# Cross attention: the copies of the two transposed halves change engines and places

## The chip, the cores and the metric

One core of a Trainium2 chip runs the whole kernel. The metric is the device time of one execution in microseconds; the time of a kernel is the median over its runs.

## The reference

The kernel computes twelve residual blocks over `x` of 128 sequences, 32 tokens and 128 features. Three of them are cross attentions of 16 heads of 8 features, in which the 32 tokens of a sequence ask a context of 257 keys. They run the function that is changed here, and differ only in the mask that is added to the scores:

```
x = x + L1_xattn(ctx, ctx, layernorm(x), mask, ...)       # one mask for all
x = x + L2_xattn(layernorm(x), ctx, ctx, key_weights, ...) # + log(weights) per key
x = x + L3_xattn(layernorm(x), ctx, tokens, 0, ...)        # keys of token 0 masked

scores = einsum('bhqd,bhkd->bhqk', Q, K) / sqrt(8) + mask
attn = softmax(scores, axis=-1)
out  = einsum('bhqk,bhkd->bhqd', attn, V)  @ Wo + bo
```

## The kernel before, in words

`xattn(name)` is called for `x1`, `x2` and `x3`. It loops over the 128 sequences, called blocks. One block has 32 tokens and 16 heads, so 512 rows of scores, in four groups of 128 partitions (an index h runs over the groups); each row has 257 keys. The keys are split for the second product into two transposed halves of 128 and one last key, which is treated apart.

The work on a block is a pipeline over several iterations. Each engine runs its own list of stages, written out by hand, in one fixed order per iteration x; the loop body is unrolled eight times, with a part before and after it. The order inside an engine is the order of the code; between engines only semaphores hold. In iteration x the engines do:

- PE: the four transposes of the first half of block x-4 into PSUM bank 6 (L1695), the four of the second half into bank 7 (L1702), K of block x into bank 4 (L1708), V of block x into bank 5 (L1711). Then it waits until bank 7 has been copied out, because three products write into the same bank: the output product (L1721, one iteration in four), the products for the last key (L1729, one iteration in four) and the product with V of block x-5 (L1740, every iteration). Last come the scores of block x-1 into banks 0 to 3 (L1751).
- DVE: four reductions of block x-2 (L1804; each adds the mask to one bank, writes the scores to SBUF and takes their maximum), with the reciprocal of the sums of block x-3 (L1816) and the copy of bank 6 for block x-4 (L1821) between the second and the third; in `x3` the masked `kT` (L1829); in two iterations of four a sum for `oT` (L1836); the evacuation of the product with V (L1846); then what follows L1721 (L1855) or L1729 (L1859).
- ACT: the four exponentials of block x-2 (L1761), the copy of bank 7 for block x-4 (L1770) between the first and the second; `kT` of block x with its bias (L1778, not in `x3`); `vs` of block x (L1781).
- POOL: the head-masked queries `qb` (L1661), the last key's weights `PB` (L1669), the scaling of a block's exponentials by the reciprocals (L1676), which releases PE's transposes.
- SP: the loads of context, mask rows and keep rows, four blocks deep.

The waits that touch the change: `pT_psum` and `pT2_psum` say that bank 6 and bank 7 hold their transposes, `pT_ready` and `pT2_ready` that they are copied into `pt`; `s_summed` counts the reductions, `exp_done` the blocks of exponentials, `av_psum` the products with V.

Of the kernel before, what the change touches and what calls it, by code (L numbers as in the profile page):

```python
# [147 lines left out]
def program(nc, T, out):  # L148

    with ExitStack() as ctx:  # L150
# [4 lines left out]
        B = [ctx.enter_context(nc.psum_tensor(f"bank{i}", [P, 512], F32)) for i in range(8)]  # L155
# [1419 lines left out]
        def xattn(name):  # L1575

            bias = name != "x3"
            with ExitStack() as c2:
# [15 lines left out]
                pt = sb2("pt", [P, 2, 2, 4 * P])  # L1594
# [160 lines left out]
                @block.scalar  # L1755
                def _(act):
                    def stages(x, r_, i, ok):
                        def exps(b, hs, j):
                            for h in hs:
                                act.wait_ge(*s_summed(4 * b + h + 1))  # L1760
                                ins = act.activation(sx[:, j, h, 0:KEYS], sx[:, j, h, 0:KEYS], ACT.Exp, bias=nm[:, j, h:h + 1], scale=-1.0,  # L1761
                                                     accum_out=sm[:, j, h:h + 1])
                            return ins
                        if ok(x - 2):
                            exps(x - 2, (0,), (r_ - 2) % 4)
                        b, q = x - 4, r_ % 2
                        if ok(b):
                            act.wait_ge(*pT2_psum(b + 1))
                            act.wait_ge(*av_psum(b - 1))
                            act.copy(pt[:, q, 1, :], B[7][:]).then_inc(pT2_ready.sem, 1)  # L1770
                        if ok(x - 2):
                            exps(x - 2, (1, 2, 3), (r_ - 2) % 4).then_inc(exp_done.sem, 1)
                        b, q = x, r_ % 2
                        if ok(b):
                            if keep is None:
                                act.wait_ge(*k_psum(b + 1))
                                act.wait_ge(*scores(4 * (b - 1)))
                                act.activation(kT[:, q, :], B[4][:, 0:KEYS], ACT.Identity, bias=v(name + "_bk")).then_inc(k_ready.sem, 1)  # L1778
                            act.wait_ge(*kv_psum(b + 1))
                            act.wait_ge(*av_psum(b - 7))  # L1780
                            act.copy(vs[:, r_, :], B[5][:, 0:2 * P]).then_inc(v_ready.sem, 1)  # L1781
                    run(act, stages)

                @block.vector
                def _(dve):
                    st_ = Steps(dve, sig, "dve_step")
                    dve.wait_ge(*last_psum(1))
                    st_.count(dve.tensor_copy(VL[:], B[7][:, 0:NB]))
                    st_.link(dve.tensor_copy(bor[:], B[7][:, P:2 * P]))
                    st_.link(dve.tensor_tensor(X[:], X[:], bor[:].unsqueeze(1).to_broadcast([P, TILES, P]), ALU.add))  # L1790
                    dve.sem_inc(last_ready.sem, 1)  # L1791
                    if name == "x1":
                        dve.wait_ge(*row_loaded(4))
                        st_.link(dve.tensor_scalar(maskq[:], maskq[:], -1.0e9, None, ALU.mult))

                    def stages(x, r_, i, ok):
                        def reduce(b, j, hs):
                            add = maskq[:] if rows is None else rows[j][:]
                            for h in hs:
                                dve.wait_ge(*scores(4 * b + h + 1))  # L1800

                                dve.sem_inc(sig.sems["dve_passed"], 1)

                                dve.tensor_tensor_reduce(sx[:, j, h, 0:KEYS], B[h][:, 0:KEYS], add, -1.0, 3.0e38, ALU.add, ALU.min,  # L1804
                                                         nm[:, j, h:h + 1]).then_inc(s_summed.sem, 1)
                        b, j = x - 2, (r_ - 2) % 4
                        if ok(b):

                            dve.wait_ge(*pT2_psum(b - 3))
                            dve.wait_ge(*pb_ready(b - 3))  # L1810
                            reduce(b, j, (0, 1))
                        b, j = x - 3, (r_ - 3) % 4
                        if ok(b):
                            dve.wait_ge(*exp_done(b + 1))
                            dve.wait_ge(*p_ready(b - 3))
                            dve.reciprocal(rs[:, j, :], sm[:, j, :]).then_inc(rs_ready.sem, 1)  # L1816
                        b, q = x - 4, r_ % 2
                        if ok(b):
                            dve.wait_ge(*pT_psum(b + 1))
                            dve.wait_ge(*av_psum(b - 1))  # L1820
                            dve.tensor_copy(pt[:, q, 0, :], B[6][:]).then_inc(pT_ready.sem, 1)  # L1821
                        if ok(x - 2):
                            reduce(x - 2, (r_ - 2) % 4, (2, 3))
                        b, q, j = x, r_ % 2, r_ % 4
                        if ok(b):
                            if keep is not None:
                                dve.wait_ge(*k_psum(b + 1))
                                dve.wait_ge(*scores(4 * (b - 1)))
                                dve.tensor_tensor(kT[:, q, :], B[4][:, 0:KEYS], keep[j][:], ALU.mult).then_inc(k_ready.sem, 1)  # L1829
                        for half, late in ((0, 9), (1, 10)):  # L1830
                            if r_ % 4 == late % 4 and ok(x - late):
                                tl, tq = (x - late) // 4 if isinstance(x, int) else i * (U // 4) + (r_ - late) // 4, (r_ - late) % 8 // 4
                                dve.wait_ge(*a_ready(4 * (tl + 1)))
                                dve.wait_ge(*pl_ready(tl + 1))
                                dve.wait_ge(*y_psum(tl))
                                ins = dve.tensor_reduce(oT[:, half * 2 * S:(half + 1) * 2 * S].rearrange("p (b s) -> p b s", b=2),  # L1836
                                                        a[:, tq, 2 * half:2 * half + 2].rearrange("p b j s -> p b s j"), AX.X, ALU.add)
                                if half:
                                    ins.then_inc(o_ready.sem, 1)
                        b, q, tq = x - 5, (r_ - 5) % 4, (r_ - 5) % 8 // 4  # L1840
                        if ok(b):
                            dve.wait_ge(*av_psum(b + 1))
                            if q == 0:
                                dve.wait_ge(*o_ready((b // 4 if isinstance(b, int) else i * (U // 4) + (r_ - 5) // 4) - 1))

                            dve.scalar_tensor_tensor(out=a[:, tq, q, 0:4, :],  # L1846
                                                     in0=B[7][:, 2 * P:3 * P].rearrange("p (j s) -> p j s", j=4),
                                                     scalar=v(name + "_bv" if bias else "zero"),
                                                     in1=const("head").unsqueeze(2).to_broadcast([P, 4, S]),
                                                     op0=ALU.add, op1=ALU.mult).then_inc(a_ready.sem, 1)  # L1850
                        if r_ % 4 == 3 and ok(x - 11):
                            tl = (x - 11) // 4 if isinstance(x, int) else i * (U // 4) + (r_ - 11) // 4
                            dve.wait_ge(*y_psum(tl + 1))
                            xt_ = X[:, bass.ds(tl, 1), :]
                            dve.tensor_tensor(xt_, xt_, B[7][:, P:2 * P].unsqueeze(1), ALU.add).then_inc(x_added.sem, 1)  # L1855
                        if r_ % 4 == 0 and ok(x - 8):
                            tl, tq = (x - 8) // 4 if isinstance(x, int) else i * (U // 4) + (r_ - 8) // 4, (r_ - 8) % 8 // 4
                            dve.wait_ge(*pl_psum(tl + 1))
                            dve.tensor_tensor(a[:, tq, :, 4, :], B[7][:, 0:P].rearrange("p (b s) -> p b s", b=4),  # L1859
                                              VL[:, bass.ds(tl * 4, 4)].unsqueeze(2).to_broadcast([P, 4, S]), ALU.mult).then_inc(pl_ready.sem, 1)  # L1860
                    run(dve, stages)
                    st_.close()

# [321 lines left out]
```

## Time and profile before

| | |
|---|---|
| median of 3 runs | 3520.45 us (3514.63 to 3530.14) |
| the profiled execution, its time | 3534.02 us |
| its span | 3532.2 us |
| PE busy | 2646.5 us (75%) |
| DVE busy | 2237.4 us (63%) |
| ACT busy | 1821.8 us (52%) |
| POOL busy | 1673.7 us (47%) |
| granted TensorE clock, mean | 0.856 |

The scores (L1751) of the three cross attentions start between 815.1 and 1243.7, 1661.5 and 2091.8, and 2636.9 and 3066.4 us of the span. The busy shares of the table are means over stages with other limits; the rows below are read from the three stretches. In a timeline each row has its start, its duration, the engine, the line and the operation, and in brackets the idle time of the engine before it and what ended it. An instruction on DVE or ACT can start up to 0.1 us before the recorded end of the one before it, so steps are taken from start to start.

### The profile page before, as it was taken

How to read it: one execution, taken by the hardware profiler on the slowest of the kernel's cores; microseconds unless marked ns; L12 is line 12 of the kernel's file. 1: busy time of each engine (PE TensorE's matmuls, PEld its weight loads, DVE VectorE, ACT ScalarE, POOL GpSimd, SP SyncE). 2: the span in 40 equal slices, each digit the busy share in tenths (PEclk: the TensorE clock that was granted, in tenths of full speed). 3: DMA queues.
4: the chain of work that ended last, by engine and by line, in shares of the span. 5: the costliest groups of instructions: out<-in, count | busy, mean ns of one | idle time of the engine just before them, and what ended most of it. 6: DMA issues, size and time to landing. Idle time of an engine off the chain costs nothing. (4 is left out here: it accounts for less than half of the span.)

```text
span 3532.2 us, 96857 instructions
## 1 busy us (share of the span) xinstructions
PE 2646.5 (75%) x27184; PEld 2121.3 (60%) x27185; DVE 2237.4 (63%) x8001; ACT 1821.8 (52%) x5775; POOL 1673.7 (47%) x1776
## 2 busy tenths in 40 slices
PE   4972577738999979847999973477749999787562
PEld 2752466626777769825777751376627777566551
DVE  4876711147888847754888877431159999878415
ACT  3441033327999933224999975023338888644110
POOL 2630055525777710001777762035527777646161
PEclk9985588969999979968999996579979999999565
DMA  2003044331111100010333320223434545300122
GB/s 83 1 1 100 14 122 119 113 91 42 39 39 39 36 8 0 31 83 27 79 78 78 78 47 6 52 86 117 115 86 118 116 116 116 75 1 1 49 84 67
DMA packets 209741, 224.97 MB, mean 64 GB/s; under 512 B 29652, under 2 KB 177620, under 8 KB 208949
## 3 DMA queue, kind: packets, MB, share of 16 engines
q1 hardware_dynamic: 196948, 197.56, 21.2%
q0 software_dynamic: 12672, 25.98, 2.9%
q8 instruction: 55, 0.90, 0.1%
q14 instruction: 66, 0.53, 0.0%
HBM read 201.68 MB, written 21.76 MB: 63 GB/s over the span
## 5 line engine op out<-in xcount | busy, mean ns | idle before, releaser
L1676 POOL TENSOR_TENSOR sx<-sx,rs 128x1028 f32<-128x1028 f32 x384 | 731.2, 1904 | 297.4 <-DVE rs L1816 297.3
L1761 ACT ACTIVATE sx<-sx,nm 128x257 f32<-128x257 f32 x1536 | 770.7, 505 | 126.0 <-DVE nm L1804 115.2
L1804 DVE CUSTOM_DVE_ANT_0 sx<-bank,rows 128x257 f32<-128x257 f32 x1024 | 393.9, 422 | 63.5 <-PE bank L1751 48.0
L1438 ACT ACTIVATE hT<-bank,B 128x128 f32<-128x128 f32 x714 | 205.5, 367 | 432.2 <-PE bank L1406 285.4
L309 POOL TENSOR_TENSOR rstd<-var,nhalf 128x16 f32<-128x16 f32 x24 | 69.7, 2904 | 654.0 <-DVE var L326 654.0
L1464 DVE TENSOR_TENSOR yb<-bank,b2s 128x128 f32<-128x128 f32 x159 | 46.4, 292 | 425.4 <-remote 218.3
L1761 ACT ACTIVATION_READ_ACCUMULATOR sx<-sx,nm 128x1 f32 x1536 | 290.4, 189 | 0.0
L1751 PE MATMUL bank<-kT,qb 32*128 32x257 f32 x3072 | 275.9, 428 | 2.7 <-DVE nm L1804 2.5
L1419 PE MATMUL bank<-W,hT 128*128 x1428 | 231.7, 309 | 59.4 <-ACT hT L1438 42.1
L1740 PE MATMUL bank<-pt,vs 128*32 128x128 f32 x6144 | 245.6, 276 | 19.6 <-ACT pt L1770 6.2
L1821 DVE COPY pt<-bank 128x512 f32<-128x512 f32 x384 | 253.6, 660 | 2.1 <-PE bank L1695 1.7
L1695 PE MATMUL bank<-C,sx 128*128 128x128 f32 x1536 | 251.9, 286 | 2.9 <-POOL sx L1676 2.9
L1419 PEld LDWEIGHTS bank<-W,hT 128*128 128x128 f32 x1428 | 202.0, 216 | 77.1 <-issue 73.7
L1711 PEld LDWEIGHTS bank<-W,ct 128*128 128x128 f32 x1536 | 235.0, 193 | 22.1 <-ACT vs L1781 1.2
L1708 PE MATMUL bank<-ct,W 128*128 128x257 f32 x768 | 235.3, 388 | 16.7 <-DVEq L1791 15.3
L1406 PE MATMUL bank<-xT,W 128*128 128x128 f32 x1428 | 238.9, 317 | 0.7 <-DMA W<-in_L_w 0.5
L1695 PEld LDWEIGHTS bank<-C,sx 128*128 128x128 f32 x1536 | 161.0, 141 | 130.6 <-issue 100.7
L1711 PE MATMUL bank<-W,ct 128*128 128x128 f32 x1536 | 236.2, 277 | 0.2 <-ACT vs L1781 0.2
L1702 PE MATMUL bank<-C,sx 128*128 128x128 f32 x1536 | 230.6, 273 | 0.0
L1804 DVE CUSTOM_DVE_ANT_0 sx<-bank,maskq 128x257 f32<-128x257 f32 x512 | 196.4, 422 | 41.0 <-PE bank L1751 32.8
L1770 ACT COPY pt<-bank 128x512 f32<-128x512 f32 x384 | 217.1, 565 | 10.1 <-PE bank L1702 10.1
L1406 PEld LDWEIGHTS bank<-xT,W 128*128 128x128 f32 x1428 | 209.9, 224 | 11.6 <-issue 3.8
(384 smaller groups left out, 5798.6 us busy)
## 6 DMA issues: line engine op xcount, KB each, us to landing
ct<-in_ctxT SPq DMA_DIRECT2D x384, 128.5 KB
W<-in_L_w SPq DMA_DIRECT2D x159, 256.0 KB
rows<-rows_x SPq DMA_DIRECT2D x256, 128.5 KB
keep<-rows_keep SPq DMA_DIRECT2D x128, 128.5 KB
yg<-copy_outs SPq DMA_DIRECT2D x40, 256.0 KB
token_rows<-XN SPq DMA_DIRECT2D x24, 256.0 KB, 2.3
W<-in_L_w SPq DMA_DIRECT2D x39, 128.0 KB
wu<-in_up_w SPq DMA_DIRECT2D x1, 4608.0 KB, 14.0
```

Of the source, the lines that this page charges most:

```text
L1406: ins = pe.matmul(B[2 + q][:, c * P:(c + 1) * P], W1[:, (r_ - 1) % 4, c * P:(c + 1) * P], xT[:, q, :], start=True, stop=True)
L1419: ins = pe.matmul(B[6 + q][:, 0:P], hT[:, q, c * P:(c + 1) * P], W2[:, bass.ds(e, 1), c, :].rearrange("p e n -> p (e n)"), start=(c == 0), ...
L1676: pool.tensor_tensor(sx[:, j, :, 0:KEYS], sx[:, j, :, 0:KEYS], rs[:, j, :].unsqueeze(2).to_broadcast([P, 4, KEYS]), ALU.mult).then_inc(p_r ...
L1695: ins = pe.transpose(B[6][:, h * P:(h + 1) * P], sx[:, j, h, 0:P], ident)
L1702: ins = pe.transpose(B[7][:, h * P:(h + 1) * P], sx[:, j, h, P:2 * P], ident)
L1708: pe.matmul(B[4][:, 0:KEYS], w(name + "_k"), ct[j][:], start=True, stop=True).then_inc(k_psum.sem, 1)
L1711: ins = pe.matmul(B[5][:, c * P:(c + 1) * P], ct[j][:, c * P:(c + 1) * P], w(name + "_v"), start=True, stop=True)
L1740: ins = pe.matmul(B[7][32 * h:32 * h + 32, 2 * P:3 * P], vs[:, j8, c * P + 32 * h:c * P + 32 * h + 32], pt[:, q, c, h * P:(h + 1) * P], st ...
L1751: pe.matmul(B[h][:, 0:KEYS], qb[p, q].rearrange("p j s -> p (j s)"), kT[p, q, :], start=True, stop=True, tile_position=(32 * h, 0)).then_i ...
L1761: ins = act.activation(sx[:, j, h, 0:KEYS], sx[:, j, h, 0:KEYS], ACT.Exp, bias=nm[:, j, h:h + 1], scale=-1.0, accum_out=sm[:, j, h:h + 1])
L1804: dve.tensor_tensor_reduce(sx[:, j, h, 0:KEYS], B[h][:, 0:KEYS], add, -1.0, 3.0e38, ALU.add, ALU.min, nm[:, j, h:h + 1]).then_inc(s_summed ...
L1821: dve.tensor_copy(pt[:, q, 0, :], B[6][:]).then_inc(pT_ready.sem, 1)
```

## The change

ACT copies bank 6 (the first half) instead of bank 7, ahead of its first exponential instead of behind it. DVE copies bank 7 instead of bank 6, behind its third reduction instead of ahead of it. The semaphores are awaited and counted by the engine that now does the copy.

```
 ACT
-                        if ok(x - 2):
-                            exps(x - 2, (0,), (r_ - 2) % 4)
                         b, q = x - 4, r_ % 2
                         if ok(b):
-                            act.wait_ge(*pT2_psum(b + 1))
+                            act.wait_ge(*pT_psum(b + 1))
                             act.wait_ge(*av_psum(b - 1))
-                            act.copy(pt[:, q, 1, :], B[7][:]).then_inc(pT2_ready.sem, 1)
+                            act.copy(pt[:, q, 0, :], B[6][:]).then_inc(pT_ready.sem, 1)
                         if ok(x - 2):
-                            exps(x - 2, (1, 2, 3), (r_ - 2) % 4).then_inc(exp_done.sem, 1)
+                            exps(x - 2, (0, 1, 2, 3), (r_ - 2) % 4).then_inc(exp_done.sem, 1)
 DVE
                             dve.reciprocal(rs[:, j, :], sm[:, j, :]).then_inc(rs_ready.sem, 1)
+                        if ok(x - 2):
+                            reduce(x - 2, (r_ - 2) % 4, (2,))
                         b, q = x - 4, r_ % 2
                         if ok(b):
-                            dve.wait_ge(*pT_psum(b + 1))
+                            dve.wait_ge(*pT2_psum(b + 1))
                             dve.wait_ge(*av_psum(b - 1))
-                            dve.tensor_copy(pt[:, q, 0, :], B[6][:]).then_inc(pT_ready.sem, 1)
+                            dve.tensor_copy(pt[:, q, 1, :], B[7][:]).then_inc(pT2_ready.sem, 1)
                         if ok(x - 2):
-                            reduce(x - 2, (r_ - 2) % 4, (2, 3))
+                            reduce(x - 2, (r_ - 2) % 4, (3,))
```

## Rows read from the trace of the kernel before

**Rows 1.** Stretches: length; busy us of PE, PEld, DVE, ACT, POOL; clock, DMA, GB/s.

```profile
830.00:1245.00 415.00, 405.69 (x4973) 313.37 (x4972) 349.89 (x1472) 389.48 (x1349) 322.19 (x368) 1.00 0.14 38
1680.00:2085.00 405.00, 397.44 (x4846) 305.55 (x4844) 341.16 (x1433) 379.36 (x1315) 313.80 (x358) 1.00 0.35 77
2660.00:3070.00 410.00, 400.40 (x4878) 307.62 (x4876) 380.47 (x1570) 339.92 (x1207) 316.56 (x361) 1.00 0.49 113
1245.00:1260.00 15.00, 6.28 (x96) 4.22 (x94) 10.02 (x37) 3.73 (x11) 4.60 (x4) 0.93 0.12 25
```

**Rows 2.** Waits, 1700 to 2000: who waited for whom, us, times, longest.

```profile
PEld bank L1740 <- ACT pt L1770: 10.3, 45, 0.2
```

**Rows 3.** Timeline of the second stage: one iteration with neither L1721 nor L1729.

```profile
1851.19 0.66 PE L1695 MATMUL bank<-C,sx 128*128 128x128 f32 x4
...
1851.44 0.43 DVE L1804 CUSTOM_DVE_ANT_0 sx<-bank,rows 128x257 f32<-128x257 f32 x1 [0.23 <-PE bank L1751]
...
1851.68 0.60 PE L1702 MATMUL bank<-C,sx 128*128 128x128 f32 x4
...
1851.91 0.51 ACT L1761 ACTIVATE sx<-sx,nm 128x257 f32<-128x257 f32 x1
1852.01 0.30 PEld L1708 LDWEIGHTS bank<-ct,W 128*128 128x128 f32 x2
...
1852.14 0.17 DVE L1816 RECIPROCAL rs<-sm 128x4 f32<-128x4 f32 x1
1852.22 0.66 DVE L1821 COPY pt<-bank 128x512 f32<-128x512 f32 x1
...
1852.42 0.57 ACT L1770 COPY pt<-bank 128x512 f32<-128x512 f32 x1
...
1853.14 0.42 DVE L1804 CUSTOM_DVE_ANT_0 sx<-bank,rows 128x257 f32<-128x257 f32 x1
1853.20 0.41 PEld L1740 LDWEIGHTS bank<-pt,vs 128*32 128x32 f32 x16 [0.23 <-ACT pt L1770]
...
1853.81 0.31 PEld L1751 LDWEIGHTS bank<-kT,qb 32*128 32x128 f32 x8 [0.20 <-DVE nm L1804]
...
1854.70 0.43 DVE L1804 CUSTOM_DVE_ANT_0 sx<-bank,rows 128x257 f32<-128x257 f32 x1 [0.23 <-PE bank L1751]
1854.73 0.36 ACT L1781 COPY vs<-bank 128x256 f32<-128x256 f32 x1
...
1855.17 0.51 ACT L1761 ACTIVATE sx<-sx,nm 128x257 f32<-128x257 f32 x1
```

**Rows 4.** Timeline of the second stage: the next two iterations, L1721 and L1729.

```profile
1855.68 0.57 ACT L1770 COPY pt<-bank 128x512 f32<-128x512 f32 x1
...
1856.37 0.30 PEld L1721 LDWEIGHTS bank<-W,oT 128*128 128x128 f32 x2
...
1858.25 0.43 DVE L1804 CUSTOM_DVE_ANT_0 sx<-bank,rows 128x257 f32<-128x257 f32 x1 [0.21 <-PE bank L1751]
...
1859.23 0.57 ACT L1770 COPY pt<-bank 128x512 f32<-128x512 f32 x1
...
1859.92 0.16 PEld L1729 LDWEIGHTS bank<-PB,C 128*32 128x32 f32 x8
...
1861.62 0.43 DVE L1804 CUSTOM_DVE_ANT_0 sx<-bank,rows 128x257 f32<-128x257 f32 x1 [0.21 <-PE bank L1751]
```

**Rows 5.** Timeline of the third stage: one iteration with neither.

```profile
2850.14 0.43 DVE L1804 CUSTOM_DVE_ANT_0 sx<-bank,rows 128x257 f32<-128x257 f32 x1 [0.21 <-PE bank L1751]
...
2851.12 0.57 ACT L1770 COPY pt<-bank 128x512 f32<-128x512 f32 x1
...
2853.42 0.42 DVE L1804 CUSTOM_DVE_ANT_0 sx<-bank,rows 128x257 f32<-128x257 f32 x1
```

**Rows 6.** Timeline of a later stage: PE's load released by a DVE evacuation.

```profile
1300.08 0.72 DVE L1165 STREAM_TRANSPOSE vt<-bank 128x512 f32<-128x512 f32 x1 [4.72 <-PE bank L1091]
...
1300.85 0.30 PEld L1082 LDWEIGHTS bank<-XNT,W 128*128 128x128 f32 x2 [0.23 <-DVE vt L1165]
```

## The prediction

> **What bounds the kernel now.** I read the page first: no engine is busy for more than 75% of the span, so no single total decides, and the chain that ended last shows only the final stage. I then went to the three stretches that run the changed code. In them TensorE's granted clock is 1.00 (the 2.4 GHz level), PE is busy for 98%, ACT for 94% of the first two, DVE for 93% of the third [rows 1]: nearly everything looks full, so the question is what one iteration waits for. The list of waits of the second stage has PE's weight loads for the product with V waiting for ACT's copy of `pt`, 45 times in 300 us, in about every second iteration [rows 2]. The timeline of one iteration shows why.
>
> An iteration of the second stage runs from one first reduction (DVE L1804, the first of four) to the next, 1851.44 to 1854.70, 3.26 us [rows 3]. Follow the releases. Reduction 0 starts at 1851.44. ACT's first exponential starts 0.47 later (1851.91), its copy of bank 7 right behind it at 1852.42 (+0.98) and ends 0.57 later, at +1.55. Bank 7 also takes the product with V, so PE loads for L1740 only at 1853.20, 0.21 behind the copy's end. The scores (L1751) stand behind that in PE's queue and start 0.61 later (1853.81); the next reduction 0 starts 0.89 behind them, released by PE. 0.47 + 0.51 + 0.57 + 0.21 + 0.61 + 0.89 = 3.26: the loop closes, and it holds no slack. ACT is nearly as tight (its last copy ends at 1855.09, 3.18 behind the exponential at 1851.91), but it is a part of the loop, not a second limit above it.
>
> The two other kinds of iteration have the same loop with one more product on bank 7 between the copy and L1740: with L1721 reduction 0 comes 1858.25 - 1854.70 = 3.55 behind the one before, with L1729 3.37 (1861.62 - 1858.25) [rows 3, 4]. Both products start 0.12 behind the end of ACT's copy (1856.25 to 1856.37, 1859.80 to 1859.92) [rows 4]. One iteration in four has the first, one the second, two have neither. In the third stage an iteration without them takes 3.28 (2850.14 to 2853.42), the copy again ending at +1.55 (2851.12 + 0.57) [rows 5].
>
> **The change part by part.** No instruction is added or removed; the semaphores keep their meaning. Two copies change engine and place, 384 of each.
>
> *Bank 7 goes to DVE, behind the third reduction.* DVE's order becomes reduction 0, reduction 1, reciprocal, reduction 2, copy, reduction 3. From [rows 3], start to start: the reciprocal at +0.70 (1852.14) behind two reductions, so a reduction hands on after 0.35; the next instruction 0.08 behind the reciprocal (1852.22), so reduction 2 at +0.78 and the copy at +1.13. DVE's copy of a bank takes 0.66, so it ends at +1.79 instead of +1.55: 0.24 later. In the third stage the reductions have the same shape and take as long, and ACT's copy ended at the same +1.55, so again 0.24 [rows 5]. The second transposes start at 1851.68 and last 0.60, done at +0.84, so the copy finds its bank ready. The following PE steps (0.21, 0.61, 0.89) are in PE's own order and don't change. Hence every kind of iteration grows by 0.24, the ones with L1721 or L1729 too, since those also start at the copy's end: 3.26 to 3.50, 3.55 to 3.79, 3.37 to 3.61.
>
> *What waits behind it on DVE.* Reduction 3 starts where it did, at +1.70 (1853.14), because one copy stood ahead of it before as well; the fourth exponential waits for it as now. The scores also wait for reduction 3: it ends at +2.12 (1853.14 + 0.42), ahead of the new scores at 1.79 + 0.21 + 0.61 = +2.61. The third stage's product with `keep`, the two sums for `oT` and the evacuation of L1740 (L1846) follow as now. In that stage DVE is full before (no wait ahead of 2853.42 [rows 5]), but with an iteration of 3.5 it has 0.2 to spare.
>
> *Bank 6 goes to ACT, ahead of the exponentials.* The first transposes start at 1851.19 and last 0.66, to 1851.85 [rows 3]. ACT's copy can start between there (+0.41) and +0.78, where DVE's copy of the same bank starts now with no wait. So the first exponential moves back to between +0.98 and +1.35. I take this at nothing: ACT's work stays 3.18 of then 3.50, so it catches up each iteration; `exp_done` is read only by the reciprocal of the next iteration, and ACT's `kT`, latest at 0.78 + 3.18 - 0.36 = +3.60, is wanted by PE's next key product, at 1852.01 - 1851.44 + 3.50 = +4.07. POOL's scaling starts from the reciprocal, which keeps its place, and gains 0.24 of slack ahead of the next transposes. If that cover were gone, ACT's 0.57 would come on top. SP's loads hang on `kv_psum`, `s_summed` and `k_ready` of three blocks earlier and are not moved.
>
> *The unknown: PE's wake from a DVE copy.* No row shows a DVE copy releasing L1740. Near rows: 0.05 from a DVE evacuation to PE's load elsewhere (1300.08 + 0.72 to 1300.85) [rows 6], and 0.12 from ACT to L1721 and L1729. Above it, PE's scores start 0.25 behind the end of reduction 3 (1853.56 to 1853.81). With 0.21 as now the term is 0.24; if DVE woke L1740 in 0.05, the plain iterations, half of all, would grow by only 0.08; with 0.25 all would grow by 0.28. I keep 0.21: the wait behind L1740 is made of several semaphores that PE passes one by one, whoever sets the last.
>
> **The sum.** Each stage has 128 blocks; the loop (copy, L1740, scores, reduction 0) is closed in 125 iterations, so 375 in three stages. 375 x 0.24 = 90 us. Against the profiled execution (3534.0 us, span 3532.2) that is 3624; that execution lies 13.6 above the median of 3520.45, so I forecast 3520 + 90 = 3610 us. Own range: low end 187 x 0.08 + 188 x 0.24 = 60, so 3580; high end 375 x 0.28 = 105, so 3625.
>
> One rule speaks against this. The Trainium skill, "Perfetto Trace Analysis", section "Identifying the Most-Contended Engine", takes for ACT and DVE the busy share as the measure and says that the engine with the highest occupancy is the one to optimize. By it ACT's 94% sets these stages, the change leaves ACT's work as it is, and the time would stay. The first rival is what that would be here.
>
> **The rivals.**
> *No change.* ACT's queue is the limit: each iteration is ACT's 3.18 plus hand-overs that don't move, because PE and DVE make up the 0.24 elsewhere. For it: in a plain iteration only 0.08 lies between ACT's last copy (1855.09) and its next exponential (1855.17) [rows 3]. Against: in the third stage ACT has no `kT` to copy and is busy for 83% [rows 1], and the iteration is just as long [rows 5]. 3520 us. Chance 6%.
> *Faster.* ACT no longer has to wait for reduction 0 before it serves PE, and runs back to back: 3.18 for a mean of (3.26 + 3.26 + 3.55 + 3.37)/4 = 3.36, so 375 x 0.18 = 68 us less, 3453. It decides from the point where DVE's copy ends before +1.55, so if the three reductions, the reciprocal and the copy took 0.24 less than the rows add up to. Nothing in the rows shortens them. Chance 4%.
> *Slower still.* The longer waits lower PE's clock, or the transposes of bank 7 come late and hold DVE's queue with reduction 3 and L1846 behind it. For the clock: a stretch with PE busy for 6.28 of 15 us was granted 0.93 [rows 1]; at that rate the PE part of the loop (0.61 + 0.89) grows by 0.11, so 375 x (0.24 + 0.11) = 131 us, 3651. Against: in the new loop PE would still be busy for nine tenths, and the transposes have 0.28 to spare. Chance 6%.
>
> **How the numbers follow.** The forecast has the remaining 84%. Range 3575 to 3640: its own range and part of the worse case; faster and unchanged are left out. A difference of 0.5% (17.6 us) is about what a measurement of this kernel can tell from none. Slower by more: 84 + 6 = 90%; within: 6%; faster: 4%.
>
> **What would show it.** In the changed kernel, from reduction 0 to the end of the bank 7 copy 1.79 instead of 1.55; L1740 released by DVE's `pt`; plain iterations of about 3.50, 3.79 with L1721, 3.61 with L1729, in all three stages alike; ACT waiting for PE's transposes and idle some 0.3 per iteration; each of the three stretches about 30 us longer and nothing else moved. It would be wrong if reduction 0 follows the copy by less than 1.71, if the copy starts before +1.1, or if the three stages change by different amounts.

## The result, and the profile after

The changed kernel takes 3639.3 us (median of 4 runs, 3637.2 to 3642.4), the kernel before, measured beside it, 3519.6 (3514.6 to 3530.1): a ratio of 1.0333 [1.0314, 1.0352], 119.8 us more. The forecast was 3610, with a range of 3575 to 3640. The direction, the place and the mechanism came as predicted; the size was about a quarter too small.

The lost time lies where it was expected. The first fence has the score loads (L1751 as before) of each of the three stages in the changed kernel: count, shortest, mean and longest ns, first to last start. The second has the middle of its second stage, in the columns of [rows 1].

```profile
L1751 PEld LDWEIGHTS bank<-kT,qb x1024: 181/184/333, 808.7 to 1276.0; 32*128 32x128 f32 x171
...
L1751 PEld LDWEIGHTS bank<-kT,qb x1024: 181/184/333, 1693.2 to 2161.8; 32*128 32x128 f32 x171
...
L1751 PEld LDWEIGHTS bank<-kT,qb x1024: 181/184/333, 2706.7 to 3172.2; 32*128 32x128 f32 x171
```

```profile
1720.00:2125.00 405.00, 366.35 (x4437) 279.93 (x4437) 323.42 (x1312) 349.59 (x1206) 287.52 (x330) 1.00 0.32 71
```

The stages last 467.3, 468.6 and 465.5 us, against 428.6, 430.3 and 429.5 before: 38.7, 38.3 and 36.0 more, 113.0 together. The two profiled executions differ by only 103.4 us in span: outside the three stages the one of before took 9.6 longer, 6.4 of it ahead of the first (815.1 us against 808.7). TensorE's granted clock is 1.00 as before, but PE's busy share has gone from 98% to 90%, ACT's from 94% to 86%: no engine has an instruction more, all of them wait more. For what, the list of waits of the second stage says (1800 to 2100; us, times, longest):

```profile
ACT pt L1768 <- PE bank L1695: 41.7, 82, 0.8
...
PEld bank L1740 <- DVE pt L1821: 20.9, 40, 0.5
```

Where PE waited for ACT's `pt` [rows 2], it now waits for DVE's, 0.5 us at a time where it was 0.2. ACT idles ahead of its copy (L1768 now), and the page's groups give the cost of both copies (busy us, mean ns of one; idle before and its releaser):

```profile
L1768 ACT COPY pt<-bank 128x512 f32<-128x512 f32 x384 | 225.4, 587 | 240.0 <-PE bank L1695 239.9
...
L1821 DVE COPY pt<-bank 128x512 f32<-128x512 f32 x384 | 263.5, 686 | 5.4 <-PE bank L1702 5.4
```

The timeline of the second stage after, a plain iteration (one without L1721 and L1729) and then DVE's copy in one with L1721 (L1802 are the reductions, L1814 the reciprocal), answers to [rows 3, 4]:

```profile
1899.61 0.43 DVE L1802 CUSTOM_DVE_ANT_0 sx<-bank,rows 128x257 f32<-128x257 f32 x1 [0.32 <-PE bank L1751]
...
1900.13 0.59 ACT L1768 COPY pt<-bank 128x512 f32<-128x512 f32 x1 [0.36 <-PE bank L1695]
...
1900.30 0.17 DVE L1814 RECIPROCAL rs<-sm 128x4 f32<-128x4 f32 x1
1900.41 0.43 DVE L1802 CUSTOM_DVE_ANT_0 sx<-bank,rows 128x257 f32<-128x257 f32 x1
...
1900.76 0.69 DVE L1821 COPY pt<-bank 128x512 f32<-128x512 f32 x1
...
1901.37 0.42 DVE L1802 CUSTOM_DVE_ANT_0 sx<-bank,rows 128x257 f32<-128x257 f32 x1
...
1901.67 0.41 PEld L1740 LDWEIGHTS bank<-pt,vs 128*32 128x32 f32 x16 [0.53 <-DVE pt L1821]
...
1902.28 0.31 PEld L1751 LDWEIGHTS bank<-kT,qb 32*128 32x128 f32 x8 [0.20 <-issue]
...
1903.17 0.43 DVE L1802 CUSTOM_DVE_ANT_0 sx<-bank,rows 128x257 f32<-128x257 f32 x1 [0.41 <-PE bank L1751]
...
1903.86 0.17 DVE L1814 RECIPROCAL rs<-sm 128x4 f32<-128x4 f32 x1
1904.07 0.43 DVE L1802 CUSTOM_DVE_ANT_0 sx<-bank,rows 128x257 f32<-128x257 f32 x1
...
1904.42 0.69 DVE L1821 COPY pt<-bank 128x512 f32<-128x512 f32 x1
...
1905.23 0.30 PEld L1721 LDWEIGHTS bank<-W,oT 128*128 128x128 f32 x2 [0.53 <-issue]
```

Read the plain iteration like the one before. Reduction 0 starts at 1899.61; DVE's copy starts 1.15 later and ends 0.69 after that, at +1.84. L1740 follows 0.22 behind, the scores 0.61, the next reduction 0 after 0.89: 3.56, against 3.26. Only the end of the copy has moved; the three legs behind it are the old ones. The second of them, 0.61, is PE's own step: [rows 3] put the scores' wait down to reduction 3, which here ends 0.49 ahead of them (1901.37 + 0.42), and the step is the same. The other kinds grow as well: over the middle of this stage the mean goes from 3.26 to 3.55 for plain iterations, from 3.36 to 3.67 with L1729, from 3.69 to 4.04 with L1721. (The forecast of 3.79 for the last rested on one iteration of 3.55, shorter than that kind is on average.)

### The profile page after: what moved, and what is told of

Same layout as the page of the kernel before. It is cut to its first block and busy times, and to the rows that moved or that the text cites. A ratio compares the mean times of both kernels' runs of the same rounds, so it can differ in the third digit from the quotient of the medians.

```text
span 3635.6 us, 96857 instructions
## 1 busy us (share of the span) xinstructions
PE 2656.5 (73%) x27184; PEld 2126.8 (58%) x27185; DVE 2268.7 (62%) x8001; ACT 1831.5 (50%) x5775; POOL 1675.0 (46%) x1776
## 5 line engine op out<-in xcount | busy, mean ns | idle before, releaser
L1676 POOL TENSOR_TENSOR sx<-sx,rs 128x1028 f32<-128x1028 f32 x384 | 731.6, 1905 | 409.6 <-DVE rs L1814 409.6
L1761 ACT ACTIVATE sx<-sx,nm 128x257 f32<-128x257 f32 x1536 | 768.0, 506 | 0.9 <-DVE nm L1802 0.9
L1802 DVE CUSTOM_DVE_ANT_0 sx<-bank,rows 128x257 f32<-128x257 f32 x1024 | 412.3, 421 | 82.2 <-PE bank L1751 74.4
L1768 ACT COPY pt<-bank 128x512 f32<-128x512 f32 x384 | 225.4, 587 | 240.0 <-PE bank L1695 239.9
L1740 PE MATMUL bank<-pt,vs 128*32 128x128 f32 x6144 | 245.6, 276 | 74.7 <-DVE pt L1821 74.7
L1761 ACT ACTIVATION_READ_ACCUMULATOR sx<-sx,nm 128x1 f32 x1536 | 294.4, 192 | 0.0
L1751 PE MATMUL bank<-kT,qb 32*128 32x257 f32 x3072 | 276.4, 429 | 2.8 <-DVE nm L1802 2.6
L1821 DVE COPY pt<-bank 128x512 f32<-128x512 f32 x384 | 263.5, 686 | 5.4 <-PE bank L1702 5.4
L1802 DVE CUSTOM_DVE_ANT_0 sx<-bank,maskq 128x257 f32<-128x257 f32 x512 | 206.6, 423 | 51.9 <-PE bank L1751 48.4
L1740 PEld LDWEIGHTS bank<-pt,vs 128*32 128x32 f32 x6144 | 158.0, 109 | 117.8 <-DVE pt L1821 106.4
```

The source lines that it names most:

```text
L1676: pool.tensor_tensor(sx[:, j, :, 0:KEYS], sx[:, j, :, 0:KEYS], rs[:, j, :].unsqueeze(2).to_broadcast([P, 4, KEYS]), ALU.mult).then_inc(p_r ...
L1740: ins = pe.matmul(B[7][32 * h:32 * h + 32, 2 * P:3 * P], vs[:, j8, c * P + 32 * h:c * P + 32 * h + 32], pt[:, q, c, h * P:(h + 1) * P], st ...
L1751: pe.matmul(B[h][:, 0:KEYS], qb[p, q].rearrange("p j s -> p (j s)"), kT[p, q, :], start=True, stop=True, tile_position=(32 * h, 0)).then_i ...
L1821: dve.tensor_copy(pt[:, q, 1, :], B[7][:]).then_inc(pT2_ready.sem, 1)
```

## The experiments

The theory: a block takes the time from its reduction 0 to the end of bank 7's copy, plus a fixed tail on PE. What counts is where in an engine's order that copy stands; which engine makes it, and what is done to bank 6, count for next to nothing. The rivals: ACT's exponentials, now behind a copy, are what is late; or the exchange of engines costs, by PE's wake or by DVE's slower copy.

**ACT copies ahead of its exponentials, but still bank 7.** One half of the change alone, on the kernel before:

```diff
-if ok(x - 2):
-    exps(x - 2, (0,), (r_ - 2) % 4)
 ... (ACT's copy of bank 7)
-    exps(x - 2, (1, 2, 3), (r_ - 2) % 4).then_inc(exp_done.sem, 1)
+    exps(x - 2, (0, 1, 2, 3), (r_ - 2) % 4).then_inc(exp_done.sem, 1)
```

> The kernel before with one part of the change alone: ACT still copies bank 7, but ahead of its four exponentials; DVE still copies bank 6 ahead of its third reduction. Theory (the iteration follows the end of the bank 7 copy, 1.54 us behind reduction 0 in the kernel before): the copy now waits for PE's second transposes, which are done near +0.85, so it starts near +0.97 as before and ends near +1.56; time 3520 to 3535 us although every exponential comes about 0.5 us later. Rival (the change costs because the exponentials stand behind a copy on ACT): most of the 120 us of the change appears here, 3590 to 3640.

3514.8 us, ratio 0.9985 [0.9976, 0.9995], 5 us below the expected range. The exponentials behind a copy cost nothing. Its timeline in the second stage (L1768 is ACT's copy of bank 7) shows a loop of 3.26 as before, the copy starting at +0.96 and ending at +1.55:

```profile
1850.56 0.43 DVE L1802 CUSTOM_DVE_ANT_0 sx<-bank,rows 128x257 f32<-128x257 f32 x1 [0.21 <-PE bank L1751]
...
1851.52 0.59 ACT L1768 COPY pt<-bank 128x512 f32<-128x512 f32 x1 [0.18 <-PE bank L1702]
...
1852.32 0.41 PEld L1740 LDWEIGHTS bank<-pt,vs 128*32 128x32 f32 x16 [0.23 <-ACT pt L1768]
...
1853.82 0.43 DVE L1802 CUSTOM_DVE_ANT_0 sx<-bank,rows 128x257 f32<-128x257 f32 x1 [0.23 <-PE bank L1751]
```

Here the copy waits for PE's second transposes and no longer for reduction 0 and an exponential. The kernel before thus has two ways of nearly the same length to the start of this copy, +0.98 through the exponential and +0.96 through PE's transposes, so taking the exponential out of the first way gains next to nothing.

**The engines exchanged, DVE's copy one place earlier.** The changed kernel, with reduction 2 behind the copy instead of ahead of it:

```diff
-reduce(x - 2, (r_ - 2) % 4, (2,))
 ... (DVE's copy of bank 7)
-reduce(x - 2, (r_ - 2) % 4, (3,))
+reduce(x - 2, (r_ - 2) % 4, (2, 3))
```

> The changed kernel with the place on DVE undone: DVE copies bank 7 ahead of reductions 2 and 3, behind the reciprocal; ACT copies bank 6 first as in the change. Theory: the copy waits for the second transposes, starts near +0.97 and ends near +1.66, 0.12 later than before; reductions 2 and 3 move back behind it, so that reduction 3 (end near +2.4) releases the scores in the plain iterations: 3.26 becomes about 3.45, with L1721 3.69 about 3.81; time 3565 to 3590 us, half of the change's cost. Rival (the engine of the copy is what costs, not its place): as the changed kernel, 3625 to 3645.

3532.2 us, ratio 1.0034 [1.0023, 1.0045]: of the 119.8 us, 107 are gone by moving the copy past one reduction. The time was missed by 33 us on the good side, for two reasons. The copy started at +0.87 and not at +0.97: bank 7 is ready soon after +0.84. And reduction 3 does not hold the scores up: it ends at +2.24, the scores start 0.15 later, and that is 0.60 behind L1740, as without it. From its timeline (L1819 is the copy):

```profile
1851.81 0.43 DVE L1802 CUSTOM_DVE_ANT_0 sx<-bank,rows 128x257 f32<-128x257 f32 x1
...
1852.68 0.69 DVE L1819 COPY pt<-bank 128x512 f32<-128x512 f32 x1
...
1853.60 0.41 PEld L1740 LDWEIGHTS bank<-pt,vs 128*32 128x32 f32 x16 [0.26 <-DVE pt L1819]
...
1853.63 0.42 DVE L1802 CUSTOM_DVE_ANT_0 sx<-bank,rows 128x257 f32<-128x257 f32 x1
1854.20 0.31 PEld L1751 LDWEIGHTS bank<-kT,qb 32*128 32x128 f32 x8 [0.20 <-DVE nm L1802]
...
1855.10 0.43 DVE L1802 CUSTOM_DVE_ANT_0 sx<-bank,rows 128x257 f32<-128x257 f32 x1
```

The copy ends at +1.56 and the iteration takes 3.29: the tail, from the copy's end to the next reduction 0, is 1.73; with ACT's copy it was 1.71 [rows 3]. Its stages last 431.4, 432.9 and 436.0 us, against 428.6, 430.3 and 429.5 before, so of the 13 us that stay the third has half. There DVE, the fullest engine but PE [rows 1], goes into reduction 0 of a plain iteration without a wait and is late with it: it starts 1.00 behind the scores and not 0.90.

**DVE's copy one place later.** The opposite edit: `reduce(..., (2, 3))` ahead of the copy.

> The changed kernel with DVE's copy of bank 7 one reduction later still, behind all four. Theory: the copy ends 0.35 later, near +2.19, and every closed iteration (375) grows by 0.35: 131 us over the changed kernel, 3770 us. Rival (the change costs through something else than the end of this copy, ACT's order or TensorE's clock): within 20 us of the changed kernel, 3620 to 3660.

3766.5 us, ratio 1.0698 [1.0680, 1.0716]: as expected. The copy ends at +2.18, L1740 comes 0.22 later, the iteration takes 3.90:

```profile
1951.07 0.43 DVE L1802 CUSTOM_DVE_ANT_0 sx<-bank,rows 128x257 f32<-128x257 f32 x1 [0.33 <-PE bank L1751]
...
1952.56 0.69 DVE L1821 COPY pt<-bank 128x512 f32<-128x512 f32 x1
1953.47 0.41 PEld L1740 LDWEIGHTS bank<-pt,vs 128*32 128x32 f32 x16 [0.88 <-DVE pt L1821]
...
1954.97 0.43 DVE L1802 CUSTOM_DVE_ANT_0 sx<-bank,rows 128x257 f32<-128x257 f32 x1 [0.42 <-PE bank L1751]
```

**The delay without the exchange.** The kernel before, ACT's copy of bank 7 one exponential later: `exps(..., (0, 1), ...)` ahead of it, `(2, 3)` behind.

> The kernel before with ACT's copy of bank 7 one exponential later, behind the second; engines, DVE's order and PE's as before. Theory: only the end of that copy counts, whichever engine makes it, so it ends 0.49 later (one exponential, start to start) and 375 iterations grow by 0.49: 184 us, 3700 us. Rival (the change costs because a DVE copy is slow to release PE, or because of DVE's order): ACT's copy a little later costs less than 60 us, 3520 to 3580.

3706.1 us, ratio 1.0516 [1.0499, 1.0534]: as expected. Nothing has changed engine here, and the loss is larger than the change's. The lines (reductions L1804, copy L1770): the copy ends at +2.03, the iteration takes 3.75.

```profile
1852.52 0.43 DVE L1804 CUSTOM_DVE_ANT_0 sx<-bank,rows 128x257 f32<-128x257 f32 x1 [0.33 <-PE bank L1751]
...
1853.99 0.56 ACT L1770 COPY pt<-bank 128x512 f32<-128x512 f32 x1
...
1854.77 0.41 PEld L1740 LDWEIGHTS bank<-pt,vs 128*32 128x32 f32 x16 [0.72 <-ACT pt L1770]
...
1856.27 0.43 DVE L1804 CUSTOM_DVE_ANT_0 sx<-bank,rows 128x257 f32<-128x257 f32 x1 [0.42 <-PE bank L1751]
```

**PE's products taken off bank 7.** If the loss is that L1740 has to wait for bank 7's copy, it should go when L1721, L1729 and L1740 write to bank 6, which ACT copies early in the changed kernel. The waits for the evacuations of these products move with them, from the second transposes to the first, and DVE reads bank 6 there (the edit is abridged):

```diff
 pe.wait_ge(*pT_ready(b))            # ahead of the first transposes (bank 6)
+pe.wait_ge(*a_ready(b - 1)), pl_ready, x_added
 ...
-pe.wait_ge(*a_ready(b - 1)), pl_ready, x_added
+pe.wait_ge(*pT2_ready(b))           # ahead of the second transposes (bank 7)
 ...
-pe.wait_ge(*pT2_ready(b + 1))       # ahead of L1721, L1729, L1740
+pe.wait_ge(*pT_ready(b + 1))
-B[7][:, P:2 * P], B[7][32 * g:...], B[7][32 * h:...]
+B[6][:, P:2 * P], B[6][32 * g:...], B[6][32 * h:...]
```

> The changed kernel, with the products L1721, L1729 and L1740 written into bank 6 instead of bank 7, so that PE waits for ACT's early copy (end near +1.1) and no longer for DVE's; the waits for their evacuation move from the second transposes to the first. Both copies stay as the change has them. Theory: the change's cost goes, because PE no longer waits for DVE's copy; what is next is reduction 3 (near +2.2), which releases the scores at about +2.45: 3.34 for all kinds of iteration, time 3485 to 3520 us. Rival (the cost is in the order of ACT or DVE itself): 3620 to 3650.

3538.8 us, ratio 1.0045 [1.0031, 1.0060], with the copies standing as in the change and DVE's copy of bank 7 ending as late (on average at +1.86 in the second stage). So 101 of the 119.8 us hung on the shared bank, as the theory says, but the time stayed 19 us above the expected range: a new wait took its place. Its waits from 1700 to 2000 (L1698 are the first transposes, L1847, L1856 and L1860 DVE's evacuations):

```profile
PEld bank L1698 <- DVE a L1860: 12.2, 22, 0.6
PEld bank L1698 <- POOL sx L1676: 11.5, 22, 0.6
PEld bank L1698 <- DVE a L1847: 10.1, 22, 0.6
PEld bank L1698 <- DVE X L1856: 9.4, 22, 0.4
```

PE now waits to refill bank 6 until DVE has emptied it of the products, where bank 7 gave that evacuation the time of the first transposes. That is so in three kinds of iteration out of four; in the fourth the last wait is the one for POOL's scaling of the exponentials (L1676).

**The same, with the evacuations as early as DVE can.** On top of the last: all four reductions ahead of DVE's copy (harmless once L1740 no longer waits for it), and the two sums for `oT` moved behind the evacuations.

> The changed kernel with the products L1721, L1729 and L1740 in bank 6 (run e4_b6_after), DVE's copy of bank 7 behind all four reductions, and DVE's sum for oT behind the evacuations instead of ahead of them. In e4_b6_after PE's first transposes waited for DVE's evacuation of the shared bank (0.58 before the transposes in a plain iteration), which stands behind the sum. Theory: both waits go, and an iteration is held by ACT's 3.2 and PE's own work: 3.2 to 3.4, time 3450 to 3495 us, faster than both kernels. Rival (the loop through the shared bank stays, now with the evacuation in it): 3520 to 3545 us.

3519.7 us, ratio 0.9982 [0.9970, 0.9994]. Another 19 us (22 by the ratios, since the kernel before took 3523.8 beside this one), and no more: the expected 3450 to 3495 was wrong, the rival's 3520 right. The same waits remain, the one for POOL too (L1835 and L1848 are evacuations here), so the loop through the shared bank is only exchanged for another of about the same length.

```profile
PEld bank L1698 <- DVE a L1835: 12.2, 22, 0.8
PEld bank L1698 <- DVE a L1848: 11.4, 22, 0.6
PEld bank L1698 <- POOL sx L1676: 10.5, 23, 0.5
```

**Bank 7's copy early on ACT, bank 6's late on DVE.** The first experiment, with `reduce(..., (2, 3))` ahead of DVE's copy of bank 6: the mirror image of the change's place on DVE, with the other bank in it, and a place later still.

> The kernel with ACT's early copy of bank 7 (run e1_act_early), and DVE's copy of bank 6 moved behind all four reductions, since PE needs that copy only in the next iteration. Theory: reduction 3 then ends near +1.6 instead of +2.1 and never releases the scores; the loop through the copy of bank 7 stays and is a little shorter than 3.26, so 3495 to 3515 us. Rival (the copy of bank 6 is on the path too): its end moves from +1.44 to about +2.2, so 3600 us or more.

3513.8 us, ratio 0.9976 [0.9965, 0.9986], inside the expected range. It is the lowest time of all, but not to be told from the first experiment's 3514.8: the intervals of the two ratios overlap. DVE's copy behind reductions costs nothing when the bank is one that PE doesn't wait for. The loop got no shorter, though, so reduction 3 was not what held it. It runs through PE's own order, as in the first experiment; PE is busy for 99% of the stretch in the second fence (columns of [rows 1]):

```profile
1800.19 0.58 ACT L1768 COPY pt<-bank 128x512 f32<-128x512 f32 x1
...
1800.99 0.41 PEld L1740 LDWEIGHTS bank<-pt,vs 128*32 128x32 f32 x16
...
1801.60 0.31 PEld L1751 LDWEIGHTS bank<-kT,qb 32*128 32x128 f32 x8 [0.20 <-issue]
...
1802.25 0.66 PE L1695 MATMUL bank<-C,sx 128*128 128x128 f32 x4
...
1802.74 0.60 PE L1702 MATMUL bank<-C,sx 128*128 128x128 f32 x4
...
1803.01 0.36 ACT L1779 COPY vs<-bank 128x256 f32<-128x256 f32 x1
...
1803.45 0.59 ACT L1768 COPY pt<-bank 128x512 f32<-128x512 f32 x1
```

```profile
1680.00:2060.00 380.00, 377.09 (x4561) 289.88 (x4554) 328.41 (x1351) 357.70 (x1240) 295.29 (x339) 1.00 0.36 78
```

From copy to copy: 0.58 for the copy, 0.22 to L1740, 0.61 to the scores, 0.65 to the next first transposes, 1.09 to the end of the second, 0.11 to the copy, together 3.26. ACT looks as if it ran back to back, with only 0.08 between `vs` and the copy, but that 0.08 is a wait for PE: in every iteration of the middle of the second stage the copy starts 0.11 behind the end of the second transposes, whether ACT has idled 0.08 until then or 0.37. Left to itself ACT is faster. In the kernel with the products in bank 6 it goes from copy to copy in 3.12 where nothing holds it:

```profile
1710.87 0.59 ACT L1769 COPY pt<-bank 128x512 f32<-128x512 f32 x1 [0.41 <-PE bank L1698]
...
1713.99 0.59 ACT L1769 COPY pt<-bank 128x512 f32<-128x512 f32 x1
```

**All together.** Means over about 100 iterations of the second stage, worked out from the timelines: end of bank 7's copy behind reduction 0, length of an iteration, and the tail, the difference of the two. (Of the tails before, a plain iteration has 1.72, one with L1729 1.82, one with L1721 2.15.) The kernel before, measured beside each, took 3519.4 to 3523.8 us.

| kernel | us | copy ends | iteration | tail |
|---|---|---|---|---|
| ACT early, bank 6 late | 3513.8 | 1.52 | 3.38 | 1.86 |
| ACT early | 3514.8 | 1.53 | 3.38 | 1.85 |
| before | 3519.6 | 1.55 | 3.40 | 1.85 |
| exchanged, DVE early | 3532.2 | 1.56 | 3.41 | 1.86 |
| after | 3639.3 | 1.85 | 3.71 | 1.85 |
| ACT late | 3706.1 | 2.03 | 3.89 | 1.86 |
| exchanged, DVE late | 3766.5 | 2.21 | 4.06 | 1.86 |

Whoever copies and in whatever order, the tail in this stage is the same to 0.01; the times follow the end of the copy. In the third it is the same to 0.02, but for the exchanged kernel with DVE early, whose 1.91 comes from DVE's late reduction 0.

## Why the prediction was right, and where its size was off

*The loop.* Right. Reduction 0, copy of bank 7, L1740, scores, reduction 0 set the iteration before, and they set it after, in all three stages nearly alike (38.7, 38.3, 36.0 us). What the prediction did not see is the second way to the copy, through PE's transposes, which is as long; the change made the first one longer, so this did not matter here.

*"DVE's copy of a bank takes 0.66 … the copy at +1.13, so it ends at +1.79 … 0.24 later."* This is the term that was mis-sized. It measured 0.31 in the first two stages and 0.29 in the third (36.0 / 125): together 114 of the 119.8 us, which is inside the interval (110 to 124). The 0.07 missing in the first two stages has three parts. The copy takes 0.686 in this place, not the 0.66 of [rows 3]: 0.03. The reduction follows the reciprocal after 0.105 (1900.30 to 1900.41) instead of the 0.08 that the copy took, and once in eight iterations after about 0.21 (1903.86 to 1904.07), so that the copy starts at +1.167 on average and not at +1.13: 0.037. The third stage has no such iterations. And the mean end before was 1.545, not 1.55. I had taken durations from rows in which the instruction stood behind another one.

*The range.* 3639.3 lies 0.7 inside its upper end, and that is luck. My own range ended at 3625; the 15 us above it were taken from "slower still", a case that did not occur.

*The unknown, PE's wake from a DVE copy.* 0.22 from the copy's end to L1740, as from ACT's (1901.45 to 1901.67; ACT's in [rows 3], 0.21). The other loads keep their own wakes as well: L1721 in the second stage 0.12 behind ACT's copy [rows 4] and 0.12 behind DVE's (1905.11 to 1905.23). So the near rows of other loads were no guide; why the loads differ was not tried. The 0.25 behind reduction 3 was no wake at all, but PE's own step, as the 0.15 of the exchanged kernel with DVE early shows.

*ACT's copy ahead of the exponentials at nothing.* Right by the first experiment. ACT idles 240.0 / 384 = 0.62 per block ahead of its copy, more than the 0.3 that I wrote: that was only the growth. Before, by the same view of the page, it idled (126.0 + 10.1) / 384 = 0.35 ahead of L1761 and L1770, so the growth is 0.27.

*The rivals.* "No change" is refuted here: ACT's occupancy fell from 94% to 86% while the time rose. The Trainium skill's rule ("Perfetto Trace Analysis", section "Identifying the Most-Contended Engine") would have put the limit on ACT; the trace shows it on a chain of releases that uses ACT only in part. "Faster" needed the copy to end before +1.55; it ended at +1.84. Its price was wrong, too: in the two experiments in which ACT serves PE ahead of its exponentials the gain is 5 and 10 us and not 68, because the copy then waits for PE's transposes. "Slower still" through the clock: 1.00 in the stretch shown, so no; through late transposes: DVE's copy idled 5.4 us in all for them, so no.

*Open.* Why the reduction starts 0.21 behind the reciprocal once in eight iterations was not tried apart (the loop body is eight iterations long, but which place of it is concerned was not followed up). Nor were products in a bank of their own, which could tell how much both loops through a shared bank cost together.

## What to carry to other kernels

When every engine looks full, close the loop: follow the releases from one instruction to the same one of the next block, and see which hand-overs add up to the iteration. An instruction on that loop costs by its place in its engine's order more than by its duration: one reduction ahead of one copy cost 3%, while the same copy of the other bank could stand behind all four for nothing. Before an early copy is hoped to gain, look for a second way to its start that is as long. A short idle ahead of an instruction can be a wait all the same: see whether its start keeps a fixed distance from what it waits for. And take a duration from a row with the same neighbour ahead of it; times 375, seven hundredths are 26 us.

## What the runs showed of the hardware

- The same DVE copy of 128x512 out of a bank takes 0.660 us behind a reciprocal (bank 6, before) and 0.686 behind a reduction (bank 7 after; bank 6 behind the four reductions, too). Behind a reciprocal with a short wait for PE it takes 0.69 (exchanged, DVE early).
- ACT's takes 0.565 behind an exponential and 0.587 behind its copy of `vs`, with a wait for PE between them or without.
- PE's load for L1740, where it is the first behind the copy of bank 7, starts 0.22 us after the copy's end, from either engine, in all the kernels of the table; L1721 in the second stage starts 0.12 after it, from either engine.
